# The third normalisation ahead of two evictions on ScalarE, and p_lo's wait behind four matmuls

## The reference, cut to what matters

```
x1 = x  + attention 0: queries and keys are two 64 x 128 projections of ctx (1024 x 1024 scores),
                       values are a 128 x 128 projection of LN(x); softmax; weighted sum
x2 = x1 + routed feed-forward of LN(x1): softmax over 8 experts gives a row's input and output
                       scales, the matrix is sign(weight), 1024 x 1024; plus a bias
x3 = x2 + attention 1: queries from LN(x2), keys from ctx (128 x 128 scores), values are ctx itself
out= x3 + low-rank mixture of LN(x3): 8 experts of rank 16, routed by softmax, times 16
```

## Time and profile before

| | |
|---|---|
| median of 3 runs | 2358.14 us (2357.36 to 2358.26) |
| profiled execution | 2354.89 us |
| its span, first to last instruction | 2353.0 us |
| mean granted TensorE clock | 0.982 of full speed |
| busy: PE, PEld, DVE, ACT, POOL | 2198.7, 1708.4, 1874.6, 1104.3, 258.9 us |
| instructions | 33856 |

### The profile page before, as it was taken

How to read it: one execution, slowest core, us unless ns; L and a number is a source line. 1 busy time by engine, 2 the same in 40 slices (tenths; PEclk the granted TensorE clock), 3 DMA queues, 4 the chain that set the end, 5 groups by cost and what they waited for, 6 DMA issues and landing times.

```text
span 2353.0 us, 33856 instructions
## 1 busy us (share of the span) xinstructions
PE 2198.7 (93%) x11102; PEld 1708.4 (73%) x11102; DVE 1874.6 (80%) x3130; ACT 1104.3 (47%) x1593; POOL 258.9 (11%) x296
## 2 busy tenths in 40 slices
PE   1997999999999999999999999999999999999986
PEld 1785777777777777777777777777777777777764
DVE  1436788888888888888888888888888888888873
ACT  2004444555554544555554544555555544555541
POOL 0000111111011111111011111111111111111100
PEclk7999999999999999999999999999999999999996
DMA  8001111111111111111111111111111111111100
GB/s 239 10 1 54 37 54 36 53 53 53 36 53 45 45 53 43 46 53 53 36 53 46 44 53 53 36 53 53 38 51 53 44 45 53 36 53 53 47 16 27
DMA packets 50217, 115.58 MB, mean 49 GB/s; under 512 B 14800, under 2 KB 23248, under 8 KB 50192
## 3 DMA queue, kind: packets, MB, share of 16 engines
q1 hardware_dynamic: 38624, 113.26, 14.5%
q10 hardware_dynamic: 11568, 1.98, 0.5%
HBM read 81.67 MB, written 16.78 MB: 42 GB/s over the span
## 4 chain that ended last, share of the span: by engine, by line
PE 85%; ACT 4%; issue 2%; DVE 2%; DMA 0%; POOL 0%; ACTq 0%; SPq 0%; POOLq 0%; DVEq 0%
PE acc L1066 15%; PE acc L1027 10%; PE shared L1040 5%; PE shared L1041 5%; PE shared L990 5%; PE scores L1010 5%; PE scores L1055 5%; PE scores L1054 5%; PE shared L1151 3%; PE acc L1023 3%; PE acc L1024 3%; PE acc L1025 3%; PE shared L1193 3%; PE shared L1135 3%; PE scores L1162 2%; PE shared L1083 2%
## 5 line engine op out<-in xcount | busy, mean ns | idle before, releaser
L878 DVE TENSOR_TENSOR p_lo<-prob,p_hi 128x1024 fp32r<-128x1024 f32 x256 | 312.3, 1220 | 105.8 <-ACT p_hi L685 88.0
L678 ACT ACTIVATE prob<-scores 128x1024 f32<-128x1024 f32 x256 | 260.5, 1018 | 229.3 <-PE scores L1055 178.1
L771 DVE TENSOR_REDUCE neg_max<-scores 128x1 f32<-128x1024 f32 x256 | 312.2, 1220 | 65.2 <-PE scores L1010 59.8
L605 POOL TENSOR_TENSOR rstd<-var_eps,minus_half 128x1 f32<-128x1 f32 x128 | 126.9, 991 | 1908.4 <-DVE var_eps L765 1908.4
L685 ACT ACTIVATE p_hi<-prob 128x1024 fp32r<-128x1024 f32 x256 | 271.3, 1060 | 42.8 <-PE acc L1066 38.6
L1027 PE MATMUL acc<-m_whole,cT_whole 128*128 128x512 f32 x512 | 255.2, 600 | 0.0
L886 DVE TENSOR_TENSOR p_sum<-p_sum,prob 128x1024 f32<-128x1024 f32 x192 | 233.9, 1218 | 0.0
L1010 PE MATMUL scores<-k_hh,q_hl 128*128 128x512 f32 x512 | 212.7, 496 | 0.0
L1040 PE MATMUL shared<-signT,y_hi 128*128 128x512 f32 x512 | 206.8, 404 | 0.4 <-ACT oscale L667 0.4
L1041 PE MATMUL shared<-signT,y_lo 128*128 128x512 f32 x512 | 203.9, 398 | 0.0
L1054 PE MATMUL scores<-q_hl,k_hh 128*128 128x512 f32 x512 | 200.9, 392 | 1.8 <-DVE q_m L860 1.4
(11 more groups left out here) (215 smaller groups left out, 4354.8 us busy)
## 6 DMA issues: line engine op xcount, KB each, us to landing
c_in<-in_ctx SPq DMA_DIRECT2D x32, 512.0 KB, 3.3
xn<-in_x SPq DMA_DIRECT2D x32, 512.0 KB, 4.1
x<-in_x SPq DMA_DIRECT2D x32, 512.0 KB, 3.3
c_val<-in_ctx SPq DMA_DIRECT2D x32, 512.0 KB, 3.5
out_x<-oscale SPq DMA_DIRECT2D x32, 512.0 KB, 2.9
q_m<-q_hl SPq DMA_DIRECT2D x32, 256.0 KB, 3.1
k_hh<-k_hh SPq DMA_DIRECT2D x32, 256.0 KB, 3.5
wq_nat<-in_L_xattn_Wq SPq DMA_DIRECT2D x4, 1024.0 KB, 10.0
```

What stands on the lines that cost most here:

```text
L678: nc.scalar.activation(prob[s % 2][:, :], scores[s % 2][:, :], ACT.Exp).then_inc(exp_ready, 1)
L771: nc.vector.tensor_reduce(neg_max[:, t:t + 1], scores[t % 2][:, :], AX_X, ALU.max, negate=True).then_inc(row_max, 1)
L878: nc.vector.tensor_tensor(p_lo[s % 2][:, :], prob[s % 2][:, :], p_hi[s % 2][:, :].bitcast(F32), ALU.subtract).then_inc(p_lo_ready, 1)
```

## The change

On ScalarE the third normalisation moves from behind cT_hi to the place before the two evictions of denominators, with its waits. On TensorE `weigh_values` waits for p_hi, issues the four matmuls that read it, then waits for p_lo and issues the two that read that. Matmuls and their order stay.

```
--- before.py
+++ after.py
@@ -708,6 +708,9 @@
                                                  bias=bqk_col[0:DQK, :]).then_inc(q_hi_ready, 1)
                             nc.scalar.activation(k_hh[DQK:P, half(h)], scores[0][DQK:P, half(h)], ACT.Identity,
                                                  bias=bqk_col[DQK:P, :]).then_inc(k_hi_ready, 1)
+                    if chain:
+                        act.wait_ge(den_done, nth(1, a, 1))
+                        normalize(3, c, xn_3, res)
                     if attend:
                         for h in range(2):
                             act.wait_ge(den_turned, nth(2, a, h + 1))
@@ -718,9 +721,6 @@
                         act.wait_ge(kw_done, nth(2, b - 1, 2))
                         nc.scalar.activation(cT_hi[:, :, :].rearrange("p t c -> p (t c)"), shared[0][:, :],
                                              ACT.Identity).then_inc(cT_hi_ready, 1)
-                    if chain:
-                        act.wait_ge(den_done, nth(1, a, 1))
-                        normalize(3, c, xn_3, res)
                     if prepare:
                         act.wait_ge(cT_done, nth(2, b, 2))
                         nc.scalar.activation(cT_whole[:, :, :].rearrange("p t c -> p (t c)"), shared[1][:, :],
@@ -1060,10 +1060,12 @@
                         pe.wait_ge(kw_ready, nth(2, a, 2))
                         pe.wait_ge(v_ready, nth(2, a, 2))
                     pe.wait_ge(p_hi_ready, nth(8, a, s + 1))
+                    for v, first in ((v_hi, s == 0), (v_lo, False)):
+                        for h in range(2):
+                            mm(acc[:, half(h)], v[:, s, :], p_hi[s % 2][:, half(h)], start=first, stop=False)
                     pe.wait_ge(p_lo_ready, nth(8, a, s + 1))
-                    for v, p, first, end in ((v_hi, p_hi, s == 0, False), (v_lo, p_hi, False, False), (v_hi, p_lo, False, s == T - 1)):
-                        for h in range(2):
-                            last = mm(acc[:, half(h)], v[:, s, :], p[s % 2][:, half(h)], start=first, stop=end)
+                    for h in range(2):
+                        last = mm(acc[:, half(h)], v_hi[:, s, :], p_lo[s % 2][:, half(h)], start=False, stop=s == T - 1)
                     last.then_inc(pv_done, 1)
 
                 def body(k, prepare, attend, chain):
```

## The result

The changed kernel takes 2392.97 us (median; 2390.17 to 2394.99), the kernel before 2357.75: the ratio is 1.0151, 95% interval 1.0133 to 1.0169, slower by 35 us. I had forecast 2364.4 us, slower by 0.27%. The direction was right, the size off by more than five times, and the time lies far outside the range.

What follows compares the result with a forecast made beforehand. TensorE's in-order stream was taken to set the time. 30 iterations x 0.21 us = +6.3 us, plus 0 for p_lo's moved wait, on 2358.14 us gave 2364.4 us (+0.27%), range 2358 to 2368 us.

Steps and rivals of the forecast that it cites:

- What the queue does: ScalarE's normalisation starts 2.05 us earlier, evictions and cT_hi queue behind it, and the delay reaches `low` and the next iteration.
- the slack of 0.41 us before L776: VectorE's wait for TensorE before copying xnT; with 0.08 of overlap it takes 0.49 of the 0.70 us delay.
- cT_hi at 1230.93: 0.70 us later than now: On ScalarE, evictions start at 1229.96 behind the normalisation, and cT_hi follows 0.97 us later, against 1230.23 now.
- the 1.14 us between the starts: ScalarE's time from a normalisation's start to the next instruction's start, used to put the evictions at 1229.96.
- such a lack of overlap: Rival: L776 held until L788's end, or no ScalarE overlap behind the normalisation; +0.3 to +0.4 us an iteration, about 2369; chance 0.07.
- the sum: L776 on VectorE 0.21 us later in each of 30 iterations, +6.3 us, plus 0 for the moved p_lo wait.
- carried its delay on undiminished: Behind `low`, TensorE's L1199 moves by 0.21 us and the whole next iteration moves with it.
- The wait of 1.70 us does not go; it changes its owner and is some 0.07 longer: TensorE's transposes of xn_3 wait for VectorE's cT_lo instead of the normalisation, starting at about 1232.31 instead of 1232.24.
- Part two: Moving p_lo's wait on TensorE frees 0.2 us at s = 6, which becomes a longer wait for kwT: 0 gained.
- The range: 2358 to 2368 us; slower by over 0.2% at 0.59, within at 0.30, faster at 0.11.

Runs made afterwards that it cites:

- run 3: Changed kernel with k_hh evicted before q_hl in each half: 2362.77 us, ratio 1.0021 to the kernel before.
- run 5: Changed kernel with the first eight of sixteen value matmuls ahead of the transposes of xn_3: 2367.03 us, ratio 1.0034 to the kernel before.
- run 2: Kernel before with only p_lo's wait moved behind four matmuls, ScalarE's order unchanged: 2357.81 us, ratio 1.0004.
- run 10: Kernel before with an added ScalarE copy of 160 columns ahead of cT_hi, nothing moved: 2399.39 us, ratio 1.0176.
- run 1: Kernel before with only the third normalisation moved ahead of the evictions, p_lo's wait as before: 2397.02 us, ratio 1.0170.
- run 6: Kernel before with k_hh evicted before q_hl, nothing else: 2353.64 us, ratio 0.9975.
- run 7: Changed kernel with ScalarE's order behind the normalisation made cT_hi, first denominators, cT_whole, second denominators: 2336.23 us, ratio 0.9906 to the kernel before.
- run 4: Changed kernel with all sixteen value matmuls ahead of the transposes of xn_3: 2384.74 us, ratio 1.0114 to the kernel before.

## Why the prediction was wrong, point by point

- **What the queue does** was right. The normalisation starts 0.09 us after `shift`, the wait for it changes its owner to cT_lo, the slack of 0.41 us before L776 is used up, L776 starts 0.09 us before L788's end, VectorE's row passes the rest on to `low`, and the whole iteration moves. Each has its row in the profile after.
- **"cT_hi at 1230.93: 0.70 us later than now"** was mis-sized: it is 0.13 more, since the first eviction can't overlap the normalisation. I took the 1.14 us between the starts from another pair, normalisation and cT_whole, and the rows had a counterexample that I didn't ask about: the normalisation itself started after cT_hi's end. Among the rivals I named such a lack of overlap, with 0.3 to 0.4 us an iteration; it is 0.27 (run 3: 0.15 with the overlap, where the sum had 0.21). The 0.06 that both lack lie behind `low`, where I carried its delay on undiminished: from its end to the first output matmul it is 0.97 us before (1238.75 to 1239.72) and 0.92 after (1526.44 to 1527.36). By itself this makes the forecast 2366 instead of 2364, as run 5 shows with its clock kept.
- **"The wait of 1.70 us does not go; it changes its owner and is some 0.07 longer"** is the step that failed. It is 0.21 longer, and above all I priced a longer idle stretch of TensorE at its length alone. The sum had no term for the granted clock, and none of the rivals had it. It is 24 of the 36.8 us between the spans, and behind the thirtieth normalisation the clock is at 1.2 GHz for 52 us instead of 39; what that has cost of the 5.9 us there, no run tests. The trace of before could have warned: its mean clock of 0.982 comes from the setup and the last iterations, where TensorE has gaps, and the loop ran at 2.4 GHz throughout with a gap of 1.70 in each iteration, so nothing there said how far that gap was from a fall. The Trainium skill (TensorE: Matmul & The Clock Gate, "HAM oscillation — how this bites in real kernels") describes a kernel whose clock falls again and again behind recurring waits; I should have made a rival of it. This case's trace shows the same return of the fall, but the waits there are of 3 to 5 us and for DMA, and here 1.91 us for VectorE were enough.
- **Part two** was right: nothing to gain (run 2), 0.2 us moved from before the weighing to before L1153.
- **The range** was built from bounds on one mechanism. The rows repeated almost to 0.01 us from iteration to iteration, which made the sum look safer than it was.

What stays open: why the clock falls in some iterations and not in others at the same stretch of 1.91 us, in 15, 18 or 20 of 29; the runs give the counts and the slide from one fall to the next, not the rule behind them. Nor does any run lie between 1.80 and 1.91 us but for single iterations (1.84 in run 10 and 1.85 in run 1, no fall). The theory of the last reader rests on runs 3, 6 and 10 and on this kernel's instructions only.

## What to carry to other kernels

Where an in-order TensorE waits once an iteration, its idle stretch is a quantity of its own: ask what the change does to its length, and put a fall of the granted clock among the rivals when it grows. Here 0.10 us more brought none, 0.21 us more brought 15 to 20. A stretch that can't be shortened can be broken up with work that is due anyway (run 5), and moving an instruction ahead pays only if what stands behind it is not the thing the other engines wait for; here cT_hi had to move with the normalisation (run 7).

## What the runs showed of the hardware

- Idle stretches of 1.55 to 1.80 us once an iteration of 66 us left the clock at 2.4 GHz; at 1.91 it fell in 15 to 20 of 29 periods, at 2.18 in 25. Idle time of 2.5 us an iteration in four pieces of at most 0.88 (run 4) left it there too. Each fall costs 1.6 us: sixteen matmuls of 128 x 128 take 3.54 us, not 1.95.
- ScalarE overlaps two instructions by about 0.1 us, or starts the second 0.03 after the first has ended. Which one it is changed with the start partition of earlier instructions: k_hh (partition 64) or q_hl (partition 0) evicted last, worth 0.13 us in each iteration.
